# Ranks from comparisons within a lane; gated rows copied raw by ScalarE and multiplied in place by GpSimd

## What is computed

```python
support = layernorm(x) @ W
r_D = sigmoid(support @ a2)
gated = r_D * support
out = segment_sum(gated[col] * edge_values[:, None], row)      # over the edges
out = out / segment_sum(edge_values * r_D[col, 0], row)[:, None]
out = relu(out) + softplus(out @ a1) * min(out, 0); x = x + elu(out)
```

## Time and profile before

| | |
|---|---|
| median of 3 runs | 1511.26 us (1510.49 to 1512.06) |
| the profiled execution | 1511.66 us, its span 1509.8 us |
| busy: TensorE, VectorE, GpSimd, ScalarE | 81%, 72%, 60%, 25% of the span |
| chain that ended last | VectorE 24%, TensorE 23%, GpSimd 22%, issue 16%, DMA 11% |
| costliest groups | gathers L781 541.8 us, L700 298.4 us on GpSimd; matmuls of the tiles 642.2 us on TensorE |

### The profile page before, as it was taken

How to read it: one execution, slowest core, us unless ns; L and a number is a source line. 1 busy time by engine, 2 the same in 40 slices (tenths; PEclk the granted TensorE clock), 3 DMA queues, 4 the chain that set the end, 5 groups by cost and what they waited for, 6 DMA issues and landing times.

```text
span 1509.8 us, 21274 instructions
## 1 busy us (share of the span) xinstructions
PE 1222.1 (81%) x6061; PEld 901.0 (60%) x6061; DVE 1089.0 (72%) x2846; ACT 371.7 (25%) x1174; POOL 900.1 (60%) x920
## 2 busy tenths in 40 slices
PE   4577668777888878668898888888888888888998
PEld 3466567776777767434565555555544555555787
DVE  9856899999999999235777676767667676664322
ACT  1343201111111001001333332323333333333232
POOL 0000177777777777767777777777777777770000
PEclk9989878888999989878899998999999999998999
DMA  8111144456555555556444446444444444441022
GB/s 258 38 52 51 42 62 129 130 132 144 146 143 138 138 136 150 136 109 121 113 115 113 112 115 118 116 114 112 116 112 116 116 111 114 113 112 44 22 76 73
DMA packets 158693, 166.46 MB, mean 110 GB/s; under 512 B 84303, under 2 KB 129251, under 8 KB 158588
## 3 DMA queue, kind: packets, MB, share of 16 engines
q0 software_dynamic: 42848, 114.59, 28.8%
q1 hardware_dynamic: 94572, 31.24, 9.0%
q10 hardware_dynamic: 21168, 19.35, 4.2%
HBM read 136.73 MB, written 28.38 MB: 109 GB/s over the span
## 4 chain that ended last, share of the span: by engine, by line
DVE 24%; PE 23%; POOL 22%; issue 16%; DMA 11%; POOLq 2%; ACT 2%; SPq 0%; DVEq 0%; ACTq 0%
PE bank L1599 22%; POOL rows L781 18%; DMA rows<-gated_rows_dram,ring_i 9%; DVE big L869 7%; POOL rows L700 3%; DVE S L1055 3%; DVE big L882 3%; DVE big L909 3%; POOLq L773 2%; DMA sorted_edges_dram<-big,idx 1%; DVE big L896 1%; DVE big L856 1%; DVE big L878 1%; ACT rows L1439 1%; DVE big L891 1%
## 5 line engine op out<-in xcount | busy, mean ns | idle before, releaser
L1599 PE MATMUL bank<-rows,S 128*128 128x257 f32 (+1 forms) x2254 | 642.2, 410 | 139.8 <-DMA rows<-gated_rows_dram,ring_i 102.0
L781 POOL DMA_INDIRECT rows<-gated_rows_dram,ring_i x564 | 541.8, 961 | 178.0 <-issue 158.9
L1599 PEld LDWEIGHTS bank<-rows,S 128*128 128x128 f32 x2254 | 413.4, 199 | 325.7 <-DMA rows<-gated_rows_dram,ring_i 192.6
L700 POOL DMA_INDIRECT rows<-gated_rows_dram,lg x294 | 298.4, 1015 | 95.7 <-issue 76.2
L1599 PE MATMUL bank<-big 128*98 128x80 f32 (+2 forms) x1741 | 196.6, 280 | 72.8 <-DVE big L909 70.4
L1599 PEld LDWEIGHTS bank<-big 128*98 128x98 f32 (+1 forms) x1741 | 192.1, 197 | 84.7 <-issue 82.5
L1223 DVE TENSOR_SCALAR S<-iota,lof,srec 128x128 f32<-128x128 f32 x637 | 178.0, 351 | 3.7 <-PE bank L1599 3.6
L688 POOL DMA_INDIRECT sorted_edges_dram<-big,idx x52 | 59.0, 1134 | 186.9 <-ACT big L1412 122.4
L1234 DVE TENSOR_TENSOR ag<-bank,ovr 128x257 f32<-128x257 f32 x49 | 20.9, 427 | 191.9 <-PE bank L1599 191.9
L1458 ACT COPY ovr<-bank 128x257 f32<-128x257 f32 x98 | 36.7, 374 | 334.7 <-PE bank L1599 322.0
L1599 PE MATMUL bank<-Wxs,xT 128*128 128x512 f32 x196 | 115.6, 720 | 0.1
(11 more groups left out here) (239 smaller groups left out, 1339.2 us busy)
## 6 DMA issues: line engine op xcount, KB each, us to landing
overflow_sums_dram<-ovr ACTq DMA_DIRECT2D x98, 128.5 KB
rows<-gated_rows_dram,ring_i POOLq DMA_INDIRECT x564, 2.8
gated_rows_dram<-rows SPq DMA_DIRECT2D x49, 128.5 KB, 2.7
ovr<-overflow_sums_dram SPq DMA_DIRECT2D x49, 128.5 KB, 2.3
out_dram<-S SPq DMA_DIRECT2D x48, 128.0 KB, 1.7
rows<-gated_rows_dram,lg POOLq DMA_INDIRECT x294, 3.1
res<-in_x_dram SPq DMA_DIRECT2D x1, 4352.0 KB
xn<-overflow_sums_dram ACTq DMA_DIRECT2D x33, 128.5 KB, 3.0
```

The costliest lines, as they stand in the source:

```text
L700: pool.indirect_dma_start(rows[:, turn(n), :], None, gtab[:, :], bass.IndirectOffsetOnAxis(ap=ring1[:, n:n + 1], axis=0)).then_inc(s_row[t ...
L781: pool.indirect_dma_start(rows[:, slot(b, u), :], None, gtab[:, :], bass.IndirectOffsetOnAxis(ap=ring_i[:, b // CH % 2, n:n + 1], axis=0)) ...
L1599: return nc.tensor.matmul(o, l, r, start=start, stop=stop, skip_group_check=True)
```

## The change

**Ranks.** The matrix lowerb now includes the lane itself (is_ge), so that TensorE's count is that of all edges of a block up to and with this lane. An edge's rank is this number less the edges of the same block that come later in its own lane. The first part is a product of the flags with the count of each block (lookup), the second comes from comparing the 16 block numbers of a half with each other (same, 512 elements) times a triangle of -1 (tri, tri2 in a bank from group 7 on). Both go into prod, now 65 slices of 32, and TensorE adds them (quads). The scan and the counts are gone; the totals are taken from the count of the last lane (lastb). ScalarE copies the counts, twice each (196 columns), to base2. The flags have no column in front of each run any more. The values are made from a second set of flags with the blocks innermost (flagsj, spread_flags).

**Gated rows.** ScalarE copies the rows of the bank with their last column as they are (lift, 257 columns) into one of eight row buffers (GB); the exponential is taken from there; TensorE waits for the copy (s_gv) and not for the gated rows. GpSimd multiplies the buffer in place by VectorE's reciprocal (gated, a tensor_scalar of 256 columns per block), and SyncE stores it. GpSimd's sends of groups 1 to 4 now stand between these.

```diff
-        flags = [carve(NB * HS, BF16) for k in range(2)]
-        flags4 = [halved(t) for t in flags]
-        reset = carve(NB * HS, BF16)
-        run = carve(NB * HS, BF16)
-        run4 = halved(run)
-        reset2 = bank[3][:, 0:25 * HS]
+        flags4 = [halved(carve(NB * HC, BF16), HC) for k in range(2)]
+        flagsj = carve(NB * HC, BF16).rearrange("p (n b) -> p n b", b=NB)
+        folded = [halved(carve(NB * HC // 2, BF16), HC // 2) for k in range(2)]
+        base2 = [carve(2 * NB, BF16).rearrange("p (h v b) -> p h v b", h=2, b=NB) for k in range(2)]
+        same = carve(HC * GC // 2, BF16).rearrange("p (i h j) -> p i h j", h=2, j=HC)
+        tri = carve(HC * HC // 2, BF16).rearrange("p (i j) -> p i j", j=HC)
+        tri2 = bank[3][:, 0:HC * HC].rearrange("p (i j) -> p i j", j=HC)
+        iota2 = bank[4][:, 3 * GC:3 * GC + NB]
         vals2 = bank[4][:, 0:2 * GC].rearrange("p (v j) -> p v j", j=GC)
         rank2 = bank[4][:, 2 * GC:3 * GC]
         buckets = halved(carve(NB * HC, BF16), HC)
-        prod = carve(NB * HC, BF16)
-        cntp = [carve(2 * NB, BF16).rearrange("p (h v b) -> p h v b", h=2, v=2) for k in range(2)]
+        prod = carve((NB + HC) * HC, BF16)
...
-        oneb = carve(1, BF16)
+        lastb = carve(1, BF16)
...
         carve = Carve(rows_t, 0, 2056)
-        Gt = carve(4 * GW).rearrange("p (k w) -> p k w", k=4)
-        scr = carve(F)
...
-            for g in range(G1):
-                for h in range(2):
-                    send(g, h)
-
-
-            for k in range(4):
-                pool.wait_ge(s_gd[k], 16 * len(range(k, NB, 4)))
+            def gated(p):
+                if not 0 <= p < NPAIR:
+                    return
+                q = p % 4 * 4
+                pool.wait_ge(s_gr, blocks(p)[-1] + 1)
+                pool.sem_inc(s_tick, 1)
+                for k, b in enumerate(blocks(p)):
+                    pool.tensor_scalar(Gt[:, b % GB, 0:F], Gt[:, b % GB, 0:F], sm[:, k, q + 3:q + 4], None,
+                                       ALU.mult).then_inc(s_gt, 1)
+
+            for h in range(2):
+                send(0, h)
+            for n in range(FIRST):
+                gated(n - 2)
+            for g in range(1, G1 + 1):
+                for i in range(PER):
+                    gated(turn_of(g, i) - 2)
+                    if g > 1 and i < 2:
+                        send(g - 1, i)
+
+
...
-            v.memset(halved(reset)[:, :, :, 0:1], 0.0)
             dve.wait_ge(s_const, 6)
             v.tensor_scalar(ident[:, :], iota[:, :], iotap[:, 0:1], None, ALU.is_equal)
-            v.tensor_scalar(lowerb, iota[:, :], iotap[:, 0:1], None, ALU.is_gt)
             v.tensor_scalar(identb, iota[:, :], iotap[:, 0:1], None, ALU.is_equal)
+            v.tensor_scalar(lastb, iotap[:, :].broadcast_to([P, 2]), float(P - 1), None, ALU.is_equal)
+            step(v.tensor_tensor(tri, iotab[:, 0:HC].unsqueeze(2).broadcast_to([P, HC, HC]),
+                                 iotab[:, 0:HC].unsqueeze(1).broadcast_to([P, HC, HC]), ALU.is_gt))
...
-                step(v.tensor_tensor(flags4[k][:, :, :, 1:HS],
+                step(v.tensor_tensor(flags4[k],
...
-                v.tensor_tensor(folded[k], flags4[k][:, :, :, 1:HC // 2 + 1], flags4[k][:, :, :, HC // 2 + 1:HS],
+                v.tensor_tensor(folded[k], flags4[k][:, :, :, 0:HC // 2], flags4[k][:, :, :, HC // 2:HC],
...
+            def spread_flags(g):
+                b = iota2 if g > G1 + 1 else iotab[:, 0:NB]
+                step(v.tensor_tensor(flagsj, hib[:, g * GC:(g + 1) * GC].unsqueeze(2).broadcast_to([P, GC, NB]),
+                                     b.unsqueeze(1).broadcast_to([P, GC, NB]), ALU.is_equal))
...
-                                        flags4[k][:, :, h, 1:HS].rearrange("p b j -> p j b"),
+                                        flagsj[:, h * HC:(h + 1) * HC, :],
                                         w.unsqueeze(2).broadcast_to([P, HC, NB]), ALU.mult)
...
-            def ranks(g):
+            def later(g):
+                hb = hib[:, g * GC:(g + 1) * GC].rearrange("p (h j) -> p h j", h=2)
+                t = tri2 if g > G1 + 1 else tri
+                step(v.tensor_tensor(same, hb.unsqueeze(1).broadcast_to([P, HC, 2, HC]),
+                                     hb.rearrange("p h i -> p i h").unsqueeze(3).broadcast_to([P, HC, 2, HC]), ALU.is_equal))
+                v.tensor_tensor(prod[:, NB * GC:(NB + HC) * GC].rearrange("p (i h j) -> p i h j", h=2, j=HC), same,
+                                t.unsqueeze(2).broadcast_to([P, HC, 2, HC]), ALU.mult)
+
+            def lookup(g):
                 k = g % 2
                 dve.wait_ge(s_bs, g + 1)
-                if g <= G1 + 1:
-                    step(v.tensor_tensor_scan(run, reset, flags[k], 0.0, ALU.mult, ALU.add))
-                else:
-                    for lo in range(0, 2 * NB, 25):
-                        n = min(25, 2 * NB - lo) * HS
-                        m = v.tensor_tensor_scan(run[:, lo * HS:lo * HS + n], reset2[:, 0:n], flags[k][:, lo * HS:lo * HS + n],
-                                                 0.0, ALU.mult, ALU.add)
-                    step(m)
-
...
-            def counts(g):
-                k = g % 2
-                if g >= 2:
-                    dve.wait_ge(s_tot, g)
-                for h in range(2):
-                    m = v.tensor_tensor(cntp[k][:, h, :, :],
-                                        run4[:, :, h, HC:HS].rearrange("p b o -> p o b").broadcast_to([P, 2, NB]),
-                                        flags4[k][:, :, h, 0:1].rearrange("p b o -> p o b").broadcast_to([P, 2, NB]),
-                                        ALU.subtract)
-                m.then_inc(s_cp, 1)
-                v.tensor_tensor(halved(prod, HC), run4[:, :, :, 1:HS], flags4[k][:, :, :, 1:HS], ALU.mult).then_inc(s_prod, 1)
+                v.tensor_tensor(halved(prod[:, 0:NB * GC], HC), flags4[k],
+                                base2[k][:, :, 0, :].rearrange("p h b -> p b h").unsqueeze(3).broadcast_to([P, NB, 2, HC]),
+                                ALU.mult).then_inc(s_prod, 1)
...
-                n, q, k = len(bs), p % 2 * 4, bs[0] % 4
+                n, q, k = len(bs), p % 4 * 4, bs[0] % GB
...
-                    if b >= 4:
-                        dve.wait_ge(s_gd[b % 4], b // 4 * 16)
+                    if b >= GB:
+                        dve.wait_ge(s_gd[b % GB], b // GB * 16)
...
-            ranks(0)
-            counts(0)
+            later(0)
+            lookup(0)
             centre()
+            spread_flags(0)
             for h in range(2):
                 values(0, h)
             quad(0)
+            later(1)
             for h in range(2):
                 hot(0, h)
             place(0)
...
-                    step(v.tensor_copy(reset2, reset[:, 0:25 * HS]))
-                ranks(g)
+                    v.tensor_copy(iota2, iota[:, 0:NB])
+                    step(v.tensor_copy(tri2, tri))
+                lookup(g)
                 pair(g, 0)
-                counts(g)
...
+                spread_flags(g)
                 values(g, 0)
                 pair(g, 2)
                 select1(tiles[1])
                 values(g, 1)
                 pair(g, 3)
                 quad(g)
+                if g + 1 < NG:
+                    later(g + 1)
                 hot(g, 0)
...
-                    act.wait_ge(s_cp, g - 1)
-                a.copy(flags4[k][:, :, :, 0], bank[0][:, 0:2 * NB].rearrange("p (b h) -> p b h", h=2)).then_inc(s_bs, 1)
+                    act.wait_ge(s_prod, g - 1)
+                    act.wait_ge(s_tot, g)
+                a.copy(base2[k].rearrange("p h v b -> p (h v b)"), bank[0][:, 0:4 * NB]).then_inc(s_bs, 1)
...
+            def lift(p):
+                for b in blocks(p):
+                    act.wait_ge(s_gm, b + 1)
+                    if b >= GB:
+                        act.wait_ge(s_gd[b % GB], b // GB * 16)
+                    a.copy(Gt[:, b % GB, :], bank[support_bank[b % 4]][:, 0:GW]).then_inc(s_gv, 1)
...
-                    act.wait_ge(s_gm, b + 1)
+                    act.wait_ge(s_gv, b + 1)
                     act.wait_ge(s_r1, 1 + (b >= parts[1][0]))
-                    if p >= 2:
-                        act.wait_ge(s_gr, (p - 1) * 2)
-                    a.activation(sm[:, k, p % 2 * 4:p % 2 * 4 + 1], bank[support_bank[b % 4]][:, F:GW], ACT.Exp,
+                    if p >= 4:
+                        act.wait_ge(s_gr, (p - 3) * 2)
+                    a.activation(sm[:, k, p % 4 * 4:p % 4 * 4 + 1], Gt[:, b % GB, F:GW], ACT.Exp,
...
-            def gated(p):
-                for k, b in enumerate(blocks(p)):
-                    act.wait_ge(s_gr, b + 1)
-                    a.activation(Gt[:, b % 4, 0:F], bank[support_bank[b % 4]][:, 0:F], ACT.Identity, bias=zcol[:, 0:1],
-                                 scale=sm[:, k, p % 2 * 4 + 3:p % 2 * 4 + 4]).then_inc(s_gt, 1)
-
             def step1(n):
```

(18 more changed lines are left out.)

## The result

| | |
|---|---|
| the changed kernel | 1522.78 us, median of 7 runs (1519.74 to 1525.07) |
| the kernel before | 1512.06 us, median of 7 runs (1510.29 to 1516.66) |
| ratio | 1.0064, 95% interval 1.0047 to 1.0081: slower by 0.64% |
| profiled executions | 1522.95 us (span 1521.1) against 1511.66 us (span 1509.8) |

The forecast was 1502 us. The third rival, slower by held issues, came true at almost its number, 1523 us, in part by luck: the stage that it priced at +34 us grew by 28.0, and the start that it shared with the forecast gave 18.1 us in place of 22.3. The way into the table is by stages, since each has its own bound. All times are us, from the two traces.

What follows compares the result with a forecast made beforehand. GpSimd's chain was taken as the bound, after the first gather's start and before the tail. 1511.7 - 3.3 - 6.9 - 3.2 - 4.5 - 4.4 + 13 = 1502 us; 1495 to 1508 at 50%, wider range 1488 to 1514.

Steps and rivals of the forecast that it cites:

- The third rival: Groups 7 to 25: GpSimd's issues held at the worst phase, 2.5 us a group, +34 us, 1523 us in all; chance 14%.
- the start: Everything up to the first gather: -17.9 us, first gather at 178 us; with group 6's -4.4 us, 22.3 us.
- What bounds the kernel: Whole kernel: time is the first gather's start, plus GpSimd's chain, plus the tail; VectorE's later savings alone are worth nothing.
- the last term, groups 7 to 25: Sort stage: lookup and same hold GpSimd's issues, 1.44 us a group for 0.73, +13 us, ends -2 and +34.
- lookup of group 1: Pairs before group 1: raw copies end TensorE's wait for gating, so this point comes 3.3 us earlier.
- group 1: Second group of the start: 26.1 us where 33.0 stood, -6.9 us.
- groups 2 and 3: Start: 26.0 us each in place of 27.6, -3.2 us together.
- group 4 to the gather: End of the start: 39.2 us to the first gather where 43.7 stood, -4.5 us.
- The 2.4 us a group: VectorE's list in groups up to 5: shorter by net about 2.4 us a group without scan and counts.
- GpSimd's multiplications: Groups of the start: 0.35 to 0.8 us each, ten in a group, 1.0 us added to a group's time.
- Group 6: Eight gathers and the scatter behind them: 15.0 us where 19.4 stood, -4.4 us (0 to -6).
- The rule of the Trainium skill: Groups 7 to 25: by it lookup and same would cost nothing, the +13 us be 0; the prediction rejected it.

Runs made afterwards that it cites:

- lookup_bank_2: The changed kernel with lookup of groups 7 to 25 reading TensorE's count in bank 0, not ScalarE's SBUF copy: 1499.1 us, ratio 0.9906.
- plain_product: As lookup_bank_2, with an added, unused product of the flags with themselves directly in front of the flags in groups 7 to 25: 1510.97 us, ratio 1.0001.
- changed_again: The changed kernel measured once more, without an edit: 1525.9 us, ratio 1.0104.
- ranks_only_3: The kernel before with the ranks' part of the change alone: 1541.67 us, ratio 1.0191; as ranks_only on a slower chip, ratio 1.0117.
- base_98: As flags_bank, with TensorE's count at 98 columns again in all groups and ScalarE making the two copies: 1487.85 us, ratio 0.9842.
- gate_act: As base_98, but ScalarE and not GpSimd multiplies the copied rows in place: 1480.93 us, ratio 0.9797.
- changed_gate_act_2: The changed kernel with ScalarE and not GpSimd multiplying the copied rows: 1517.99 us, ratio 1.0054.
- flags_bank: As lookup_bank_2, with the flags of groups 8 to 25 comparing with 49 numbers in a bank, not 1568 in SBUF: 1492.05 us, ratio 0.9867.

## Why the prediction was wrong

**What bounds the kernel**: right. GpSimd's chain sets the time; each microsecond of held issues in the groups 7 to 25 came out as one of the stage in lookup_bank_2 and in plain_product.

**The step that failed** is the last term, groups 7 to 25: +13 forecast, +28.0 measured. Its working took the loss of one encounter as the rest of lookup less 0.13 us, mean 1.03, a fold of 0.29 behind it and 0.12 for same, 1.44 a group. The rule was read off the product of the kernel before, behind which the issue had been let in at once. The rows of the same trace also showed the other case: the scatter at 184.55 was not let in behind any of the first three of four products in a row, it ended 0.8 us behind the fourth (183.60 + 5.86), and the gather at 203.46, which began beside the first of two products, ended 0.8 behind the second:

```profile
202.88 2.98 DVE L869 TENSOR_TENSOR big<-big 128x784 f32<-128x784 bf16 x2
```

The prediction read each of these runs as one instruction. Behind lookup the issue is mostly not let in: to the rest of lookup comes the whole of the flags, 0.96 less the overlap of 0.08, and the fold then misses the next issue. That is 1.03 + 0.88 = 1.9, and with same 2.0; measured are 38.6 / 19 = 2.03. The third rival had the price of the worst phase, 2.5 a group, and the point from which it decides, 1.9; what took the kernel beyond that point was not a bad phase of single holds but two holds in one. Held time alone gives 26.8 - 13 = 13.8 us of the 20.8 by which the forecast missed. The chance of 14% was too low for a mechanism of which every part was visible.

**The start**: -14.3 for -17.9. The parts: lookup of group 1 came 2.4 us earlier, not 3.3; group 1 gave 3.5, not 6.9; groups 2 and 3 gave 4.4, not 3.2; group 4 to the gather 4.0, not 4.5. The first miss lies in front: the pairs begin at 40.65 in place of 38.72, for which 0.3 stood. VectorE's list there isn't longer, it is busy for 32.4 of the first 40 us where it was 36.9. It waits for TensorE, 3.05 and 1.41 us, which it didn't before, and TensorE's two wide counts, 2.98 us each for 1.56, stand ahead of what it waits for:

```profile
17.91 2.98 PE L1617 MATMUL bank<-big,lg 128*128 128x196 bf16 x8 [0.50 <-ACT big L1422]
22.64 0.76 DVE L958 SCALAR_TENSOR_TENSOR S<-bank,S 128x256 f32<-128x256 f32 x2 [3.05 <-PE bank L1617]
30.17 0.53 DVE L912 TENSOR_REDUCE big<-bank 128x32 f32<-128x352 f32 x1 [1.41 <-PE bank L1617]
```

So VectorE reaches the hot rows of group 0 at 31.80 in place of 29.87, and with them TensorE's last work ahead of the pairs. The prediction had no wait there. This beginning varies, too: 40.0 us in changed_again and 44.3 in lookup_bank_2, with the same program. The second is TensorE's clock. From 60 to 180 us the mean granted clock was 0.84, before 0.91. The windows of 10 us from 60 us on, TensorE busy, granted clock in the fourth place, of the changed kernel:

```profile
60.00:70.00 10.00, 6.20 (x23) 0.62 0.25 85
70.00:80.00 10.00, 7.31 (x32) 0.84 0.19 63
80.00:90.00 10.00, 9.23 (x63) 0.69 0.12 41
90.00:100.00 10.00, 8.89 (x55) 1.00 0.09 29
```

The clock has two levels, 1.2 and 2.4 GHz; a share of 0.62 to 0.84 is a stretch with both in it. TensorE had been busy for 9.5 of 10 us before the first of these rows (the window from 50 us). The 33.0 us of group 1 before held such a stretch, and the 25.1 set against them were counted at full clock. How much of the miss is the clock's isn't measured. The gain in groups 2 and 3 was larger than forecast, which fits pairs that came every 2.2 us and not 2.6. The working for group 4 has a slip: its parts, 24 + 1.7 + 1.6 + 0.4, give 27.7 us and not 28.7. The 2.4 us a group that the prediction worked out for VectorE's shorter list are no term of its sum, and ranks_only_3 shows that this list alone bought nothing at the start.

**GpSimd's multiplications**: 0.35 to 0.8 us was the range, 0.9 the length alone. This is also above the estimate from the Trainium skill (GPSIMD Engine Reference, section 3.1), 0.4 us. The mean was 1.46. Their price before the first gather is small or none: 2.3 us from base_98 to gate_act, nothing from changed_again to changed_gate_act_2 (183.3 in both), both within the scatter of that column. The price that no row of before could show was elsewhere: every later gather some 5 ns longer, the 3.1 us of the main stage and the 1 to 2 us that the sort stage grew beyond its held time.

**Group 6**: right, 15.6 for 15.0. **The lengths of lookup, of the values and of the wide count, and VectorE's room**: right.

**The rule of the Trainium skill** that was weighed, that tensor_tensor with two operands in SBUF does not stall the writing of descriptors ("SBUF — State Buffer", Who interferes with whom, there called inferred), would have made lookup cost nothing here. One edit shows the cost: moving one operand of that one tensor_tensor into a bank took 27.1 us off the stage. Whether GpSimd is held while it writes descriptors or while it reads the gather's indices, which lie in SBUF, no run here separates, so what fails is the price drawn from the inference; the inference itself is not tested. The same section's rule that a VectorE instruction with at most one SBUF input, outside the 2-port modes, leaves GpSimd alone agrees with the banks tried here (held time 3.0 us in flags_bank, nearly all of it beside the fold and "same", which read SBUF alone).

## What to carry to other kernels

Where GpSimd's issues are the bound, count for each VectorE instruction not its length but whether it reads two operands from SBUF, and put one of them in PSUM, even if VectorE gets slower by it. Price a run of such instructions without a gap as one long one: an issue caught by the first may leave only behind the second. And before crediting a shorter list, ask on which engine's list the stage ends: here the ranks' part saved time on VectorE in two stages in which TensorE and GpSimd set the pace.

## What was not expected of the hardware

A held issue is let in behind one VectorE instruction or behind the next; both are seen, each with the same 0.82 us to its end, and what chooses is open. In a program that contains GpSimd multiplications of 256 columns, GpSimd's gathers took 965 to 972 ns in the main stage in place of 957 to 961, hundreds of microseconds behind the last multiplication; on a slower chip 978 to 984 in place of 970 to 974. Why is open. And chips differ: two took 1732 and 1734 us for the kernel that others run in 1511, and there the ratio of the same edit differed by up to 1.2% (ranks_only 1.0070 and 1.0117 there, 1.0191 elsewhere).
